# Wide heads of a fused perceiver stack: softmax rows turned on VectorE, keys loaded from DRAM per sequence, mixing in four 32-row tiles

## What is computed

```python
def xattn(context, x):                       # L0_xattn, L2_xattn
    xn, ln = layernorm(context), layernorm(x)
    q = heads(ln @ Wq)                       # 16 or 8 heads, 64 queries each
    k, v = split(concat([xn, ln]) @ Wkv)     # 192 keys
    attn = softmax(q @ k.T * scale)
    return (attn @ v) @ Wout
x = x + xattn(ctx_1024, layernorm(x))
x = x + ...                                  # ten other blocks: scans, narrow heads, experts
```

## Time and profile before

| | us |
|---|---|
| median of 3 runs | 2430.18 (2424.86 to 2434.6) |
| the profiled execution | 2427.39 |
| its span, first to last instruction | 2425.6 |
| PE busy | 2312.0 (95%) |
| DVE busy | 1490.3 (61%) |
| ACT busy | 1163.5 (48%) |
| POOL busy | 916.8 (38%) |

### The profile page before, as it was taken

How to read it: one execution, slowest core, us unless ns; L and a number is a source line. 1 busy time by engine, 2 the same in 40 slices (tenths; PEclk the granted TensorE clock), 3 DMA queues, 4 the chain that set the end, 5 groups by cost and what they waited for, 6 DMA issues and landing times.

```text
span 2425.6 us, 41921 instructions
## 1 busy us (share of the span) xinstructions
PE 2312.0 (95%) x16426; PEld 1567.8 (65%) x16426; DVE 1490.3 (61%) x4040; ACT 1163.5 (48%) x2998; POOL 916.8 (38%) x853
## 2 busy tenths in 40 slices
PE   9999989999989999999999999999999999999998
PEld 6766656666766665666666675666666666666665
DVE  6457566666575567666564567756665555665653
ACT  5544334555445533445644453545555445354543
POOL 5334353433234336434332444543323243544310
PEclk9999999999999999999999999999999999999999
DMA  5000000000000000000000000000000000000000
GB/s 235 1 1 1 1 14 1 10 1 27 1 1 1 1 1 10 18 10 1 19 1 1 1 1 5 10 14 10 10 5 1 1 1 1 1 1 1 2 1 14
DMA packets 6821, 26.57 MB, mean 11 GB/s; under 512 B 864, under 2 KB 992, under 8 KB 5984
## 3 DMA queue, kind: packets, MB, share of 16 engines
q1 hardware_dynamic: 6624, 23.89, 2.7%
HBM read 21.79 MB, written 2.10 MB: 10 GB/s over the span
## 4 chain that ended last, share of the span: by engine, by line
PE 75%; DVE 16%; issue 3%; ACT 3%; POOL 3%; DMA 0%; POOLq 0%; DVEq 0%; SPq 0%
PE ps L486 9%; PE ps L499 8%; PE ps L549 7%; PE ps L518 6%; PE ps L510 4%; PE ps L889 4%; PE ps L628 4%; PE ps L603 3%; PE ps L471 3%; PE ps L596 3%; PE ps L650 3%; PE ps L601 3%; PE ps L677 2%; PE ps L846 2%; DVE P L1405 2%
## 5 line engine op out<-in xcount | busy, mean ns | idle before, releaser
L1919 POOL TENSOR_TENSOR P<-P,small 128x384 f32<-128x384 f32 x384 | 316.1, 845 | 564.0 <-DVE small L1430 564.0
L1140 ACT ACTIVATE P<-ps,small 128x192 f32<-128x192 f32 x768 | 315.0, 425 | 134.3 <-DVE small L1422 132.8
L1892 POOL TENSOR_TENSOR small<-small,mhalf 128x4 f32<-128x4 f32 x112 | 126.5, 1130 | 511.9 <-DVE small L1410 255.2
L499 PE MATMUL ps<-kvT,big 128*128 128x192 f32 x1536 | 311.4, 333 | 4.5 <-DVE big L1439 1.8
L499 PEld LDWEIGHTS ps<-kvT,big 128*128 128x128 f32 x1536 | 248.8, 190 | 74.9 <-issue 45.1
L1422 DVE TENSOR_REDUCE small<-ps 128x2 f32<-128x384 f32 x384 | 208.3, 550 | 108.8 <-PE ps L499 100.4
L486 PEld LDWEIGHTS ps<-wts,P 128*128 128x128 f32 x1920 | 232.3, 192 | 45.3 <-issue 30.6
L486 PE MATMUL ps<-wts,P 128*128 128x128 f32 x1920 | 247.8, 278 | 3.8 <-DVE P L1827 2.1
L2009 POOL TENSOR_TENSOR P<-T 128x512 f32<-128x512 f32 x96 | 125.4, 1306 | 197.2 <-DVE T L1709 128.2
L518 PEld LDWEIGHTS ps<-value,big 128*128 128x128 f32 x1536 | 178.6, 192 | 28.3 <-issue 18.6
L518 PE MATMUL ps<-value,big 128*128 128x128 f32 x1536 | 188.0, 278 | 0.1
(11 more groups left out here) (287 smaller groups left out, 4495.6 us busy)
## 6 DMA issues: line engine op xcount, KB each, us to landing
ctok<-ctok_dram SPq DMA_DIRECT2D x8, 512.0 KB, 4.1
ctxT<-ctx_dram SPq DMA_DIRECT2D x8, 512.0 KB, 4.1
wts<-weights_dram SPq DMA_DIRECT2D x1, 2530.0 KB, 23.3
wts<-weights_dram SPq DMA_DIRECT2D x1, 2189.0 KB, 17.8
X<-x_dram SPq DMA_DIRECT2D x8, 256.0 KB, 3.5
big<-fold_dram SPq DMA_DIRECT2D x2, 1024.0 KB, 8.5
out_dram<-X SPq DMA_DIRECT2D x8, 256.0 KB, 2.3
wts<-weights_dram SPq DMA_DIRECT2D x1, 1536.0 KB, 25.8
```

Of the source, the lines that this page charges most:

```text
L499: m = pe.matmul(ps[s][:, at:at + KEYS], big[s][:, BANK * b + 128 * p:BANK * b + 128 * p + 128], kvT[s][:, keys_at(b):keys_at(b) + KEYS], s ...
L1140: m = act.activation(probs(s, b // 2)[:, to:to + KEYS], ps[s][:, at:at + KEYS], ACT.Exp, bias=small[s][:, 4 * e + p:4 * e + p + 1], accum_ ...
L1892: pool.tensor_tensor(rstd(s, name, n), variance(s, name, n), mhalf[:, 0:n], ALU.pow).then_inc(*sig("rstd", s))
L1919: m = pool.tensor_tensor(view, view, over(small[s][:, at:at + 2], 2, [128, 2, KEYS]), ALU.mult)
```

## The change

- **Turning.** A sequence's probabilities now lie alone in 768 columns of `P` (`probs(s, b)`, two buffers instead of two for pairs). DVE turns each 32x32 block in place of PE's transposes, one `dve.transpose` of 128x768 a sequence, into two further buffers of `P` (`probs_T`). The evacuations of the turned rows go.
- **Keys.** Query `32 r + q` of a 32-row group ends as column, key `32 c + k` as partition `32 r + k` for every row group r. So the mixing needs the 192 keys of a sequence as 6 chunks of 32 rows, repeated on the four groups of 32 partitions. When a layer's `kv` is ready, SP stores `T` to DRAM (12 DMAs), waits, and for each sequence loads 32 rows x 768 columns four times (`load_rows`), into one of two buffers that overlay `T` (`kv_rows`). The load for sequence m waits until `mixed` m - 2.
- **Mixing.** For each of 6 chunks and each row group r one matmul with 32 rows of the array, weights 32x128, 128 moving columns, accumulated in bank r: 24 matmuls for a sequence instead of twelve transposes and four 512-column matmuls for a pair. The two sequences of a pair share the four banks (columns 0 to 255), so all four banks must be free of scores when a pair is mixed, and the scores of the next pair wait for the evacuation (`evacuated`).
- **Output.** `out_of` writes 128 columns of bank 0 for one tile at a time, and DVE adds each tile by itself (96 adds of 128x128 instead of 24 of 128x512).
- **Around it.** `w2`, a part of the weights, is now loaded within SP's woven list, behind the first stores; centring of the weights takes two banks instead of three. All merge lists (`ORDER`) are new: 2258 steps instead of 2498 on PE, 1549 instead of 1741 on ACT, 2118 instead of 2030 on DVE, 610 as before on POOL, 237 instead of 26 on SP.

```diff
+        def kv_rows(s, b):
+            return T[s][:, 768 * (b % 2):768 * (b % 2) + 768]
+        def mix_out(s, r, e):
+            return ps[s][:, BANK * r:BANK * r + 256].rearrange("p (h e q) -> p h e q", e=2, q=32)[:, :, e, :]
         def score_bank(g, b, hf):
-            return hf + (2 if b == (0 if g == 1 else 1) else 0)
+            return hf + 2 * ((b + (g == 1)) % 2)
...
+                def load_rows(s, k, b):
+                    for r in range(4):
+                        sp.dma_start(kv_rows(s, b)[32 * r:32 * r + 32, :], kv_dram[s][k][b].rearrange("k c d -> k (c d)"))\
+                          .then_inc(kv_loaded[s][b % 2], 16)
+                def stores(s, i, layer):
+                    yield
+                    sp.wait_ge(*(on("kv", s, i, "x2.ctx") if layer else on("kv", s, i - 1, "kv.ctx")))
+                    store_context(s, layer)
+                    yield
+                    sp.wait_ge(*(on("kv", s, i, "x2.lat") if layer else on("kv", s, i - 1, "kv.lat")))
+                    store_latents(s, layer)
+                    yield
+                    sp.wait_ge(kv_stored[s], 16 * 12 * (2 * i + layer + 1))
+                    load_rows(s, layer, 0)
+                    load_rows(s, layer, 1)
+                def loads(s, i, layer):
+                    first = 16 * layer
+                    for m in range(first + 2, 24 if layer else 16):
+                        yield
+                        sp.wait_ge(*on("mixed", s, i, m - 2))
+                        load_rows(s, layer, m % 8)
...
+                    def mix(b):
+                        m = 8 * g + b
+                        pe.wait_ge(kv_loaded[s][b % 2], 16 * 4 * (12 * i + m // 2 + 1))
+                        pe.wait_ge(*on("pT", s, i, m))
+                        turned = probs_T(s, b).rearrange("p (h c q) -> p h c q", h=4, q=32)
+                        for c in range(KEYS // 32):
+                            for r in range(4):
+                                at = slice(32 * r, 32 * r + 32)
+                                last = pe.matmul(mix_out(s, r, b % 2), kv_rows(s, b)[at, 128 * c:128 * c + 128],
+                                                 turned[at, :, c, :], start=(c == 0), stop=(c == KEYS // 32 - 1))
+                        last.then_inc(*sig("mixed", s))
...
-                    for j in range(PAIRS):
...
+                    for k in range(1, PAIRS):
+                        if k > 1:
+                            yield
+                            evacuated(k - 2)
+                        for b in (2 * k, 2 * k + 1):
+                            yield from next_scores(b, 0)
+                            yield from next_scores(b, 1)
+                        if k > 1:
+                            yield
+                            pe.wait_ge(*on("exped", s, i, 2 * (8 * g + 2 * k + (g == 1))))
+                            out_of(k - 2)
+                        yield
+                        pe.wait_ge(*on("exped", s, i, 2 * (8 * g + 2 * k + 1) + 1))
+                        mix(2 * k - 2)
+                        yield
+                        mix(2 * k - 1)
...
+                    def turn_p(b):
+                        m = 8 * g + b
+                        yield
...
+                        dve.wait_ge(*on("p_ready", s, i, m))
+                        if b > 1:
+                            dve.wait_ge(*on("mixed", s, i, m - 2))
+                        dve.transpose(probs_T(s, b), probs(s, b)).then_inc(*sig("pT", s))
+                    for k in range(1, PAIRS + 1):
+                        yield from turn_p(2 * k - 2)
+                        yield from turn_p(2 * k - 1)
+                        if k < PAIRS:
+                            yield from negmax(2 * k, 0)
...
+                        dve.wait_ge(*on("mixed", s, i, 8 * g + 2 * k - 1))
+                        if k > 1:
+                            add_out(k - 2)
+                        dve.tensor_copy(mixed_at(s, k - 1, 0), mix_halves(s, 0)).then_inc(*sig("head_dve", s))
```

More of the change, by code:

```diff
@@ L353, in build @@
         x_stored = [sem(f"x_stored{s}") for s in range(SLOTS)]
+        kv_stored = [sem(f"kv_stored{s}") for s in range(SLOTS)]
+        kv_loaded = [[sem(f"kv_{k}{s}") for k in ("even", "odd")] for s in range(SLOTS)]
+        kv_dram = [[nc.dram_tensor(f"kv_dram{s}{k}", (GB, 32, KEYS // 32, D), f32).ap() for k in range(2)] for s in range(SLOTS)]
         chain = sem("chain")
@@ new lines, in loads @@
+                def loads(s, i, layer):
[4 more added lines that the diff above has]
+                        load_rows(s, layer, m % 8)
+                def program(s):
+                    yield
+                    yield from stores(s, 0, 0)
+                    if s:
+                        yield
+                        sp.wait_ge(folded, 3)
+                        sp.dma_start(wts[:, W_AT["w2"][0]:W_N], weights[:, W_AT["w2"][0]:W_N]).then_inc(w_main, 16)
@@ L404, in program @@
                             sp.dma_start(res(s, i + 1), x[:, to:to + GT]).then_inc(x_loaded[s], 16)
+                        yield from loads(s, i, 0)
+                        if i < PASSES - 1:
                             to = ((i + 1) * SLOTS + s) * GC
@@ L409, in program @@
                             sp.dma_start(ctok[s][:, :], ctok_in[:, to:to + GC]).then_inc(ctok_loaded[s], 16)
+                        yield from stores(s, i, 1)
+                        yield from loads(s, i, 1)
+                        if i < PASSES - 1:
                             yield
@@ L412, in program @@
                             sp.dma_start(ctxT[s][:, :], ctxin[:, to:to + GC]).then_inc(ctx_loaded[s], 16)
+                            yield from stores(s, i + 1, 0)
                         yield
@@ L451, in _ @@
                     sp.wait_ge(ctx_loaded[s], 16 * PASSES)
+                    for k in range(2):
+                        sp.wait_ge(kv_loaded[s][k], 16 * 4 * 12 * PASSES)
             def rows(s, name, j, hh):
@@ L517, in out_of @@
                             at = 128 * block_of(h0 + k, nh)
[L518 to L519 removed]
+                            from_ = 1024 * t + 512 * (k % 2) + 128 * (k // 2)
+                            m = pe.matmul(out_part(s), big[s][:, from_:from_ + 128], value[:, at:at + 128],
+                                          start=(k == 0), stop=(k == 7))
                         return m
```

235 lines of the change are left out of this document (96 added, 139 removed).

## The result

| | before | after |
|---|---|---|
| median, us | 2427.55 (2424.86 to 2434.6, 4 runs) | 2460.37 (2453.8 to 2463.66, 4 runs) |
| ratio to before, 95% interval | | 1.0139 (1.0118 to 1.0159) |
| span of the profiled execution | 2425.6 | 2452.0 |
| PE busy / not busy in the span | 2312.0 / 113.6 | 2240.8 / 211.2 |
| mean granted clock of TensorE | 0.991 | 0.969 |

What follows compares the result with a forecast made beforehand. PE was taken to bound the kernel throughout. From 2427.4 us: -116 (PE) +15 (added wait) +4 (DMAs) +6 (start) = -91, 2336, plus 3 for the median: 2339 us; range for 8 in 10, 2298 to 2430.

Steps and rivals of the forecast that it cites:

- What bounds the kernel: Whole program: PE bounds it all the way in a fixed order; what leaves PE's stream shortens time nearly one to one.
- PE's stream: Mixing on PE: a pair falls from 4.29 to 3.08 us, 1.21 less for 96 pairs, -116 us.
- DVE, "both lie beside PE's work": DVE's turnings and adds, together +133 us busy, and ACT's 116 us less: both hidden beside PE's work.
- The added wait, +15: All four banks shared by scores and mixed rows: a slot's round takes 9.0 instead of 8.0 us; +15, bounds 0 and +48.
- Detour and start, +4 and +6: Key stores and row loads through DRAM: hidden but for 4 us; later first mixing at the start +6, from 0 to 8.
- Merge lists, 0 +- 20: New merge lists: not priced by the trace, taken as 0 with a bound of 20 us to either side.
- (a): Mixing on PE: row tiles run side by side only in twos, +256 us, 2595; chance 0.05.
- (c): Mixing on PE: a step of four takes longer than one of two, 0.143 us, losing 74 us: 2413; chance 0.07.
- (d): DVE's turning runs at half rate, 1.9 us each: 2385; chance 0.11.
- (e): No idle time is added and the new lists fill better: 2304; chance 0.11.
- (b): Wait on `kv_loaded` before a mixing: rows arrive late, 1.4 us a pair, +134, 2473; chance 0.09.

Runs made afterwards that it cites:

- b_halfmix: Kernel before with every mixing matmul on 256 instead of 512 columns, 125 us less on PE; 0.9796 of before, -50 us.
- b_addturn: Kernel before with four unneeded DVE transposes of 128x320 added per pair, DVE 175 us more busy; 1.0366 of before, +89 us.
- b_trade: Kernel before with 256-column mixing matmuls (PE less 125 us) and two unneeded DVE transposes a pair (DVE more 84); 0.9984 of before, -4 us.
- a_two_early: Kernel after, a quarter of the mixing, waiting only for the even sequence's exponentials; 0.9896 of before, 11 us (ratios) or 7 (medians) below its later-waiting control.
- a_nodram: Kernel after without the detour through DRAM: no key stores, row loads or waits on them; 1.0081 of before, 14 us below after.
- a_noturn: Kernel after with DVE's transpose cut from 768 to 32 columns, all but the first two; 1.0065 of before, 18 us below after.
- a_fill3: Kernel after with dummy matmuls filling 0.8 of each PE idle stretch of 0.9 us or longer; 0.9938 of before, 2414 us.
- a_start: Kernel after with the w1 weights (2530 KB) loaded behind the first key stores instead of ahead; 1.0117 of before, +28 us.

## Why the prediction was wrong

- **What bounds the kernel: the step that failed.** "What leaves PE's stream shortens it nearly one to one as long as the other slot's steps still fill the holes." 95% busy and 75% of the chain were read as leave to do so. b_halfmix gives 0.4 (50 of 125 us). The 16% of the chain that were DVE's say that PE's list is touched by DVE again and again; with less work between two touches PE only comes to the wait earlier. Of 91 us of forecast gain some 70 (0.6 of 116) were never there.
- **PE's stream** itself was right: 2.89 us a pair to the next start against 3.08. Busy time fell by only 71 us, not 116; with the clock held up in both kernels, and less the dummies, it fell by 111.
- **DVE, "both lie beside PE's work": wrong.** The price of a turning was right (960 ns), the sum too high (+88 us where 133 were computed, ACT -100 against -116), and the weight was wrong: 0 assumed, 0.4 to 0.5 in b_addturn. Taking the turning out again gave 0.14 of its time. The two differ by place and by direction. A likely reason, not shown, is that work added to a fixed order delays all behind it, while work taken out leaves the other waits standing. b_trade puts PE's gain and DVE's load together, and it is a draw.
- **The added wait, +15:** not refuted. a_two_early shows 7 to 11 us for it in a reduced kernel, at the edge of the noise.
- **Detour and start, +4 and +6:** a_nodram gives 14. The place was partly wrong: the start is late by nine us, mainly through a layer norm for which PE waits ahead of the first mixing.
- **The clock: missing from the sum.** The trace of before had it (0.991), and the prediction named the clock nowhere. b_halfmix also waits for 55 us more than before and keeps its clock (0.990); in after 20 waits are longer than 2 us, 65.9 us in all against 21.3 in b_halfmix, and what the clock takes is worth 35 us more than in before. That turned a draw into a loss of 34 us.
- **Merge lists, 0 +- 20:** open, and the main suspect for the long waits, which stay when the turning, the detour and the adds are taken out. Nothing here separates the lists from the banks that they serve; other lists for the same steps weren't tried.
- **Rivals.** (a), (c) and (d) fell by their rows, (e) by PE's idle time, which grew. (b), which ended slower, had the wrong mechanism: PE waited for loaded rows for 3.5 us in all (8.7 with the weight loads). (a) ended slower as well, and the chance for slower (0.13) was theirs alone; none of the rivals asked what the time does if PE isn't the bound after all. In (c) four starts of 0.11 by three are 0.147, not 0.143, which would have made it 2422; nothing else hangs on it.

The effects overlap and are not a sum: PE's idle time feeds the clock, so that b_trade, a draw, is at 1.2 GHz for 45 us more than before (a_noturn for 14 less than after, a_nodram for no less). What the runs show is that with the clock held up in both kernels they differ by 4 us at most, and with it left alone by 34 us.

## What to carry to other kernels

In a program whose order is fixed, busy shares near 100% don't make an engine the only bound. Before costing a trade between two engines, take a like amount from the one and add it to the other by hand, and read the two weights; here they were 0.4 and 0.4 to 0.5, so a trade of 116 us for 88 was a draw. And count the idle stretches of PE by length, not only in sum: a long one is paid for again in the clock, and cheap work in it can be worth more than the work that was saved.

## What the hardware showed that I had not expected

- 118 us of dummy matmuls, placed where PE waited, made a kernel 49 us faster (a_fill3; mean clock 0.969 to 0.998). A mixing of 96 records took 4.36 us mostly at 1.2 GHz and 2.96 at 2.4.
- Four 32-row tiles of 128 columns side by side take no longer than one full-array matmul of the same columns: 24 steps in 2.96 us with tail, 0.11 a step, as one of the 128x128 transposes of the earlier trace rows (four in 0.44). The factor of 3.07 that the Trainium skill gives for 512 columns (TensorE: Matmul & The Clock Gate, Measured speedup vs the span model) doesn't show at this size.
- A store of 64 KB costs SP 0.45 us to issue (median) and 1.3 us at the start, with megabytes of weights ahead of it in the queue (8 in 10.76 us); with 2530 KB fewer ahead, in a_start, it is 0.87 (8 in 6.94 us). From issue to landing the median of all 192 is 1.8 us.
- DVE's transpose of 32x32 blocks in f32 takes 960 ns for 768 columns and 511 for 320 (b_addturn), so 1.0 ns a column and some 190 ns more.

```profile
L1455 DVE STREAM_TRANSPOSE spare<-score x96: 511/511/514, 35.3 to 2357.5; 128x320 f32<-128x320 f32 x96
```
